# Inverse roots of 22 of the 24 norms on GpSimd, by a power and one Newton round, in a four-layer transformer kernel

## The reference

```python
# layer 0: attention with 16 heads, causal; feed-forward of 1024; gate per sample
h = layernorm(x); x1 = x + attn(h) @ Wo + bo; h2 = layernorm(x1)
x = x + g * (x1 + gelu(h2 @ W1 + b1) @ W2 + b2 - x)
# layer 1: adapter of 64 features, one of 16 experts per sample, then a norm
x = layernorm(up(expert(gelu(down(x)))) + x)
# layer 2: feed-forward of 1024, one of 8 experts per sample, then a norm
x = layernorm(gelu(x @ Wi[e] + bi[e]) @ Wo[e] + bo[e] + x)
# layer 3: adaptive norm, attention with a bias of (4, 16, 512, 512) and a key mask, feed-forward
x = ln(x) * (1 + scale) + shift; x = x + attn(x, bias, mask) @ Wo + bo; x = x + ff(ln(x))
```

## Time and profile before

| | |
|---|---|
| runs of the kernel | 1150.39 us median of 3 (1149.09 to 1150.68) |
| the profiled execution | 1148.26 us, span in the trace 1146.2 us |
| TensorE matmul busy | 1001.6 us, 87% |
| VectorE busy | 703.7 us, 61% |
| ScalarE busy | 694.9 us, 61% |
| GpSimd busy | 235.7 us, 21% |
| copies of units (planner) | 275 on ScalarE, 237 on VectorE |
| mask pairs (planner) | 83 on TensorE, 45 on GpSimd |

### The profile page before, as it was taken

One profiled execution on the slowest core, in us unless ns is written; L12 is line 12 of the kernel. 1 busy time (PEld: TensorE's weight loads), 2 busy tenths in 40 slices (PEclk: granted clock), 3 DMA queues, 4 the chain that ended last, 5 costly groups with the idle time before them and its releaser, 6 DMA issues.

```text
span 1146.2 us, 22123 instructions
## 1 busy us (share of the span) xinstructions
PE 1001.6 (87%) x7746; PEld 663.6 (58%) x7834; DVE 703.7 (61%) x1964; ACT 694.9 (61%) x1608; POOL 235.7 (21%) x362
## 2 busy tenths in 40 slices
PE   4878889798889898899789899899897999899868
PEld 3445556455546566466556476566574657657545
DVE  5668773745855747945772757746738764764750
ACT  3556665673765765675665757676656775675731
POOL 8300020000320240530040000630720170080000
PEclk9889999998999999999999999999999999999989
DMA  6878425115162454854735128667385487944500
GB/s 170 222 161 199 75 74 111 39 47 102 36 140 75 90 174 129 187 200 125 143 94 113 38 93 182 206 179 195 113 204 171 139 204 234 230 138 174 176 1 18
DMA packets 118351, 154.78 MB, mean 135 GB/s; under 512 B 12956, under 2 KB 80924, under 8 KB 118244
## 3 DMA queue, kind: packets, MB, share of 16 engines
q1 hardware_dynamic: 113636, 147.04, 48.3%
q0 software_dynamic: 1936, 3.97, 1.3%
q10 hardware_dynamic: 2672, 2.36, 0.6%
HBM read 134.47 MB, written 18.88 MB: 134 GB/s over the span
## 4 chain that ended last, share of the span: by engine, by line
PE 54%; DVE 19%; ACT 16%; issue 10%; DMA 0%; DVEq 0%; ACTq 0%
PE bank L1337 15%; PE bank L1326 9%; PE bank L1433 8%; PE bank L1288 5%; PE bank L1447 5%; PE bank L1412 3%; DVE mrow L1169 3%; DVE bias L1178 3%; ACT gT L901 3%; ACT bias L854 3%; PE bank L1302 2%; ACT prob L851 2%; PE bank L1312 2%; ACT L901 2%; ACT pT L862 2%
## 5 line engine op out<-in xcount | busy, mean ns | idle before, releaser
L854 ACT ACTIVATE bias<-bias,mrow 128x512 f32<-128x512 f32 x256 | 184.0, 719 | 191.6 <-DVE mrow L1178 189.5
L1178 DVE CUSTOM_DVE_ANT_0 bias<-bank,bias 128x512 f32<-128x512 f32 x256 | 175.5, 687 | 195.9 <-PE bank L1412 91.6
L851 ACT ACTIVATE prob<-bank,mrow 128x128 f32<-128x128 f32 (+3 forms) x256 | 134.9, 528 | 194.6 <-DVE mrow L1169 193.1
L1169 DVE TENSOR_REDUCE mrow<-bank 128x1 f32<-128x128 f32 (+3 forms) x256 | 124.1, 486 | 169.0 <-PE bank L1418 167.8
L1433 PE MATMUL bank<-ident,bias 128*128 128x128 f32 x1024 | 157.5, 277 | 37.4 <-ACT pT L862 29.5
L1433 PEld LDWEIGHTS bank<-ident,bias 128*128 128x128 f32 x1024 | 122.2, 142 | 111.3 <-ACT bias L854 56.8
L1326 PE MATMUL bank<-hT,w 128*128 128x512 f32 x384 | 181.7, 604 | 1.3 <-ACT hT L878 1.0
L1412 PE MATMUL bank<-ks,qs 128*128 128x512 bf16 (+3 forms) x425 | 143.5, 338 | 40.1 <-ACT prob L851 34.5
L1337 PE MATMUL bank<-w,gT 128*128 128x256 f32 x768 | 174.3, 381 | 0.0
L1337 PEld LDWEIGHTS bank<-w,gT 128*128 128x128 f32 x768 | 142.5, 190 | 20.2 <-issue 2.7
L821 POOL TENSOR_TENSOR bias<-bias,negmask 128x256 f32<-128x256 f32 x180 | 118.4, 690 | 127.0 <-DMA bias<-in_fside_Bx16xSxS 124.7
(11 more groups left out here) (157 smaller groups left out, 1136.5 us busy)
## 6 DMA issues: line engine op xcount, KB each, us to landing
bias<-in_fside_Bx16xSxS SPq DMA_DIRECT2D x128, 512.0 KB, 4.3
w<-in_L_cond_W SPq DMA_DIRECT2D x16, 1024.0 KB, 5.4
qs<-q_parts SPq DMA_DIRECT2D x30, 384.0 KB, 10.4
ks<-k_parts SPq DMA_DIRECT2D x30, 384.0 KB, 12.0
q_parts<-parts SPq DMA_DIRECT2D x80, 128.0 KB
k_parts<-parts SPq DMA_DIRECT2D x48, 128.0 KB
w<-in_L_cond_Wi SPq DMA_DIRECT2D x4, 1024.0 KB, 4.9
w<-in_L_cond_Wo SPq DMA_DIRECT2D x4, 1024.0 KB, 5.6
```

What stands on the lines that cost most here:

```text
L851: act.activation(prob_of(U), score_bank[U % 2][:, 0:n], ACT.Exp, bias=mrow[:, U % ROW_RING:U % ROW_RING + 1], accum_out=rsum[:, U % ROW_RI ...
L854: act.activation(prob_of(U), prob_of(U), ACT.Exp, scale=-1.0, bias=mrow[:, U % ROW_RING:U % ROW_RING + 1], accum_out=rsum[:, U % ROW_RING: ...
L1169: v.tensor_reduce(m, score_bank[U % 2][:, 0:n], AX_X, ALU.max, negate=True).then_inc(max_done, 1)
L1178: v.tensor_tensor_reduce(out=prob_of(U), in0=score_bank[U % 2][:], in1=prob_of(U), scale=-1.0, scalar=3e38, op0=ALU.add, op1=ALU.min, accu ...
```

## The change

For all norms but (0, 0) and (1, 0), given as (sample, k), the steps 2 to 12 leave VectorE. In slot 0 of tick t+2 a step `spread_of` runs the four aggregations, waits for them, and adds eps. GpSimd, at the start of its own tick t+2 and ahead of that tick's masking, waits for that sum and runs five instructions on 128x4: the power -0.5, three that make the Newton factor, and the product. Each of the first four is waited for before the next. VectorE waits for the root where it first reads it. A constant tile of -0.5 is one more memset in GpSimd's start. Since the list of steps is shorter, the planners decide anew; neither `spread_of` nor `inverse_root` has a cost in `V_LOAD`.

```diff
+ROOT_ON_DVE = [(0, 0), (1, 0)]
@@ plan_norm
-    for i in range(RSQRT_STEPS):
-        at(t + 2 + i // SLOTS, f"v{i % SLOTS}", "rsqrt", s, k, i)
+    if (s, k) in ROOT_ON_DVE:
+        for i in range(RSQRT_STEPS):
+            at(t + 2 + i // SLOTS, f"v{i % SLOTS}", "rsqrt", s, k, i)
+    else:
+        at(t + 2, "v0", "spread_of", s, k)
+        at(t + 2, "p", "inverse_root", s, k)
@@ GpSimd
+            const(pool.memset(minus_half[:], -0.5))
...
+            def rooting(ins):
+                rooted[0] += 1
+                ins.then_inc(root_step, 1)
+                pool.wait_ge(root_step, rooted[0])
+
+            def inverse_root(s, k):
+                pool.wait_ge(norm_var, ROOT[s, k] + 1)
+                var, guess, scaled = nwt[:, 0, :], nwt[:, 1, :], nwt[:, 2, :]
+                rooting(pool.tensor_tensor(guess, var, minus_half[:], ALU.pow))
+                rooting(pool.tensor_tensor(scaled, guess, var, ALU.mult))
+                rooting(pool.tensor_tensor(scaled, scaled, guess, ALU.mult))
+                rooting(pool.tensor_scalar(scaled, scaled, -0.5, 1.5, ALU.mult, ALU.add))
+                pool.tensor_tensor(rstd, guess, scaled, ALU.mult).then_inc(root_done, 1)
...
             for U in range(FIRST, LAST + 1):
+                for step, args in steps.get(U, []):
+                    if step == "inverse_root":
+                        inverse_root(*args)
                 V = U + MASK_AHEAD
@@ VectorE
+            def spread_of(s, k):
+                v.wait_ge(vec, count[0])
+                for t in range(NT):
+                    count[0] += 1
+                    v.bn_aggr(mv[:, t, :], stats[:, t, :]).then_inc(vec, 1)
+                chain[0] = count[0]
+                v.wait_ge(vec, chain[0])
+                if ROOT[s, k]:
+                    v.wait_ge(root_done, ROOT[s, k])
+                v.tensor_scalar(nwt[:, 0, :], mv[:, :, 1], 1e-12 if k == 4 else 1e-5, None, ALU.add).then_inc(norm_var, 1)
@@ apply
+                if k in (0, 1, 6) and (s, k) not in ROOT_ON_DVE:
+                    v.wait_ge(root_done, ROOT[s, k] + 1)
```

More of the change, by code:

```diff
@@ L290 @@
 NTH = {(s, k): sum(1 for x in TURN if x[1] == k and TURN[x] < n) for (s, k), n in TURN.items()}
+ROOT = order("p", "inverse_root", lambda a: a)
 FFN = order("pe", "hidden", lambda a: a[:2])
@@ L428, in build @@
         norm_rows_t = sb("norm_rows_t", [P, 4, NT])
+        minus_half = sb("minus_half", [P, NT])
         rstd, nwt = norm_rows_t[:, 0, :], norm_rows_t[:, 1:4, :]
@@ L514, in build @@
         up_done = sem("up_done")
+        norm_var = sem("norm_var")
+        root_step = sem("root_step")
+        root_done = sem("root_done")
         vec = sem("vec")
@@ L799, in res_l3 @@
                 res_landed()
+            rooted = [0]
+            def rooting(ins):
[10 more added lines that the diff above has]
+                pool.tensor_tensor(rstd, guess, scaled, ALU.mult).then_inc(root_done, 1)
             def mask_load(m):
@@ L839, in _ @@
                 for step, args in steps.get(U, []):
-                    do[step](*args)
+                    if step != "inverse_root":
+                        do[step](*args)
         @block.scalar
@@ L1207, in _ @@
             steps = dense_steps("v")
-            do = {"stats": stats_of, "rsqrt": rsqrt, "apply": apply, "apply_late": apply_late,
+            do = {"stats": stats_of, "spread_of": spread_of, "rsqrt": rsqrt, "apply": apply, "apply_late": apply_late,
                   "feature_half": feature_half, "rest": rest_of, "lo": lo, "v": values_out, "residual": residual,
@@ L1492 @@
 CONST_IDENT = 2
-CONSTS = CONST_IDENT + 7
+CONSTS = CONST_IDENT + 8
 SETUP_SCALE = 2
```

## The result

The changed kernel takes 1131.61 us (median of 4 runs, 1130.09 to 1132.46) against 1150.54 us (median of 4, 1149.09 to 1151.49): ratio 0.9835, 95% interval 0.9818 to 0.9852. That is 18.9 us less where 9.6 were forecast, and just under the range's lower end of 1132. The profiled execution took 1131.03 us with a span of 1128.9, 17.3 us shorter than that of before.

The account below looks back on a forecast made before the run. VectorE was taken to set the pace in eleven windows around norms; their 16.0 us times 0.6 gave 9.6 us, so 1150.4 - 9.6 = 1141 us. Its own range was 1136 to 1146, the wider one 1132 to 1152.

Parts of the forecast that it names:

- eleven full windows: Stretches around norms between 216 and 1006 us where VectorE is nearly always busy, so its short steps are on the path.
- the discount: Factor 0.6 on the windows' 16.0 us, for chain share, loop of waits and second engine, leaving 9.6 us.
- The sum of 16.0 us: Upper bound on the gain, added window by window over the full windows, less returning copies and capped by second engines.
- their terms: Gains priced per full window before the 0.6: 1.75 us undisturbed, less where a copy joins or a second engine caps.
- The chain's "eight tenths": In the window of 272.7 us the chain of waits counts 1.40 of the short steps' 1.75 us.
- What 228 and 370 hold: Windows of 472.2 and 798.2 us, priced at 1.07 us (a copy joins) and 1.75 us before the 0.6.
- The copies: 37 copies go from ScalarE to VectorE and 11 back, returning some 15 us to VectorE, mostly where it has room.
- GpSimd's root: Ready about 2.1 us after the sum (ends 1.6 to 3.1), power 0.7 us; on time, last norm gains nothing.
- GpSimd can no longer run ahead past a norm's tick: GpSimd's masking waits behind the root; four ticks remain for a root and one pair, so costed at nothing.
- Contention: Rival, 14%: GpSimd's five new instructions hold VectorE's two-input ones, 1.0 us in each of eleven windows; time 1150 us.
- VectorE's busy time: Sign in the profile after: down from 703.7 to about 676 us, 43 less and 15 back.

Follow-up runs that it names:

- e3: Kernel before with the root on GpSimd only for the eleven norms of the full windows, old table of copies: 1129.24 us, ratio 0.9827.
- e4: Kernel before with the root on GpSimd only for the other eleven norms, old table of copies: 1150.71 us, ratio 1.0013.
- e12: Kernel before, root on VectorE, with the masks of seven pairs (units 232 to 239, 378 to 383) on TensorE instead of GpSimd: 1142.2 us, ratio 0.9934.
- e6: Kernel before, root on VectorE, plus five unread root-like instructions on GpSimd at the same ticks for 21 norms: 1154.98 us, ratio 1.0037.
- e7: Changed kernel with GpSimd's power replaced by a 128x4 product, so the root is a constant: 1134.67 us, ratio 0.9853.
- e13: Changed kernel with old table of copies, last norm's root on VectorE, and masks of nine pairs on TensorE: 1130.73 us, ratio 0.9826.

## Why the prediction was wrong, point by point

The forecast said faster, and that was right; the size was half. The mechanism (short steps on the path of eleven full windows) was right too. Two terms of the sum were mis-sized, the discount and what two windows hold.

- **Which windows are full, and which norms count.** Right: the eleven bring everything (e3), the other eleven nothing (e4). No single view said it; the windows of a few ticks did.
- **The sum of 16.0 us.** Near the 18.3 us of the eleven windows, but by two errors that cancel. Nine of the windows gave 11.1 us where their terms make 13.2. Windows 228 and 370 gave 7.2 where the terms make 2.8.
- **The discount, "another eight tenths for the loop and the second engine. That is 0.6 x 16.0".** This step failed. It left the nine windows 7.9 of their 13.2 us, and 11.1 came, more than eight tenths: a miss of 3.2 us. In norms 138, 145 and 395 nearly the full 1.75 us came. The chain's "eight tenths" (1.40 of 1.75) was no part that stays behind: the very window it was read from, that of norm 138, gave 1.7. The 0.6 was argued from a mechanism and measured by no row (0.8 x 0.8 is 0.64, besides).
- **What 228 and 370 hold.** This step failed by more: with the discount they had 1.7 us, and gave 7.2. The steps were priced at 0.16 us each, though the earlier trace rows had 0.59 in this very window; e12 shows that ending the collisions alone brings these windows 6.5 us.
- **The clock.** Not in the sum. Behind 114 and 255 the changed kernel gains 2.2 us; ahead of 114 it loses 1.6 by a fall that the kernel before didn't have. Whether the norm of 114 has a part in either is open.
- **The copies.** Their number was right. They cost 1.9 us in ticks 318 to 330, where nothing was charged.
- **GpSimd's root.** 2.41 us instead of 2.1, the power 1.03 instead of 0.7, within the ends; on time in all 21 norms inside the units. The last norm lost 0.2 us.
- **"GpSimd can no longer run ahead past a norm's tick ... I cost it at nothing."** No masking was late, but two that had been done early moved onto the norm of 190 and stretched VectorE's pair there, 0.6 us, and in e6 and e7 it cost 4 to 6.
- **Contention.** The rival had it in the new short instructions. In e6 ten windows lose at most 0.7 us each and 1.0 us together; the one large loss, 5.8 us, is by the masking that they hold back.
- **VectorE's busy time.** About 676 us was the sign; it is 682.5. Over half of the difference is in the stretched two-input instructions.

From the forecast's 9.6 to the 17.3 us of the profiled execution: 3.2 us more in the nine windows, 5.5 in the two, 2.2 behind 114 and 255, less 1.9 for the copies of ticks 318 to 330 and 1.6 for the clock ahead of 114; small differences elsewhere add 0.3.

## What to carry to other kernels

Cut the trace into windows of a few ticks. Where one engine is busy 95% and the others well under that, an instruction taken from it is worth up to its whole length as measured there; cap it by the second engine's busy time. In nine windows here that came to 11.1 of 13.2 us, so a large discount beyond the cap needs a row that shows it. Then look for instructions in the same window that take several times their usual length beside another engine's work: ending that can be worth more than the work that is moved, and was had here for seven entries of a table. Once VectorE had been relieved in another way, the same move gave nothing (e13). Last, an engine that now waits for another does its own other work later, so ask what that work will run beside.

## What the runs showed of the hardware

- GpSimd's power on 128x4 took 1.03 us, its products 0.20 there when nothing interfered.
- A VectorE instruction with two SBUF inputs is stretched beside GpSimd's two-input masking: 0.16 to 0.55-0.66 us for 128x4, 0.48 to as much as 1.0 for 128x256. The Trainium skill ("SBUF — State Buffer", section "Who interferes with whom") gives this as an exclusive lock for one instruction; the 0.59 us of the earlier trace rows fits that, being its own 0.16 and less than one masking piece of 0.69. Two short instructions with one tile as input were stretched in that window as well: L1041 took 0.63 us and L1045 0.55 instead of 0.17.
- If it begins while GpSimd issues a DMA with masking behind it, it took 3.25 to 3.29 us (e6, e7), past four maskings and not one. A lock for one instruction alone would let it in after the first; why it didn't is open.
- TensorE's granted clock fell to 0.50 behind some of the stretches in which it idled beside a full VectorE (busy 0.91 us from 222 to 224 us, before 226 to 228 reads 0.50), and each fall cost 1.4 to 1.6 us where it could be compared. The same stretch was followed by no fall in e4. The Trainium skill ("TensorE: Matmul & The Clock Gate", section "HAM oscillation — how this bites in real kernels") warns of idle gaps between matmuls; the traces agree that the clock falls behind idling, though TensorE had work in every 2 us here (5.03 of 8.30 us in that window of the earlier trace rows).
